# An attention and mixture-of-experts layer on one core: one product moved to GpSimd, GELUs in a row, first scan ahead of the statistics

## The reference

```
x = x + layernorm(linear_attention(layernorm(x)))
x = x + layernorm(moe(layernorm(x)))

linear_attention: q, k, v = x @ W_qkv + b      16 heads of 8; q, k = elu(.) + 1 + 1e-4
    per token t, along the sequence:
    kv_s += k_t (outer) v_t ;  k_s += k_t
    out_t = (q_t . kv_s) / (q_t . k_s + 1e-6)  then @ W_out + b_out

moe: shared = gelu(x @ Wfc_s + b) @ Wproj_s + b          hidden 512
     routed = the two experts of 8 with the largest softmax(x @ Wr), each
              gelu(x @ Wfc[e] + b) @ Wproj[e] + b, weighted by their probabilities
```

## Time and profile before

| | us |
|---|---|
| median of 3 runs (lowest, highest) | 401.99 (401.25, 403.97) |
| the profiled execution, its own time | 400.21 |
| its span in the profile | 398.4 |
| TensorE busy in the span | 338.0 (85%) |
| VectorE busy | 303.1 (76%) |
| ScalarE busy | 262.3 (66%) |
| GpSimd busy | 247.9 (62%) |

### The profile page before, as it was taken

The page is one execution under the profiler, slowest core; times in us unless marked ns, Lnnn a source line. Parts: engine busy times, 40 slices in busy tenths (PEclk is TensorE's granted clock), DMA queues, the critical chain, the costliest instruction groups (busy, mean ns, idle before and its releaser), DMA issues.

```text
span 398.4 us, 8675 instructions
## 1 busy us (share of the span) xinstructions
PE 338.0 (85%) x2551; PEld 298.5 (75%) x2551; DVE 303.1 (76%) x737; ACT 262.3 (66%) x665; POOL 247.9 (62%) x338
## 2 busy tenths in 40 slices
PE   6648489698787896977989789999999999999990
PEld 2326458587576684965958689999999999997990
DVE  5699999898998989989999447766656666662283
ACT  4758474885967849679473797556666666664682
POOL 6851282575885747748547577777766666667061
PEclk9959779999999999999999999999999999999995
DMA  7563986248074340611501897999898888821883
GB/s 198 173 160 96 213 155 204 61 120 226 8 224 115 98 139 0 203 34 61 177 3 46 251 314 219 248 280 289 266 318 250 243 248 251 255 95 54 248 273 113
DMA packets 53493, 69.03 MB, mean 173 GB/s; under 512 B 6349, under 2 KB 37370, under 8 KB 53466
## 3 DMA queue, kind: packets, MB, share of 16 engines
q1 hardware_dynamic: 48628, 59.11, 52.7%
q0 software_dynamic: 4544, 9.35, 7.0%
q10 hardware_dynamic: 294, 0.26, 0.3%
HBM read 40.06 MB, written 18.15 MB: 146 GB/s over the span
## 4 chain that ended last, share of the span: by engine, by line
PE 43%; ACT 18%; DVE 11%; issue 9%; DMA 7%; POOL 5%; SPq 4%; ACTq 1%; DVEq 0%; POOLq 0%
PE bO L1304 7%; PE bS L1304 6%; PE bO L1116 5%; DVE KV L1448 4%; DMA xb<-expert_lists 3%; ACT xn L722 2%; POOL expert_lists L599 2%; DVE KV L1442 2%; ACT shared L722 2%; ACT shared L768 2%; ACT shared L737 2%; ACT SH L996 2%; PE bV L1279 2%; PE bV L1280 2%; PE bV L1281 2%
## 5 line engine op out<-in xcount | busy, mean ns | idle before, releaser
L687 POOL DMA_INDIRECT expert_results<-yb,yrow x78 | 84.2, 1080 | 34.6 <-issue 18.5
L599 POOL DMA_INDIRECT expert_lists<-rows,pos x64 | 66.4, 1037 | 21.0 <-issue 21.0
L1448 DVE TENSOR_TENSOR_SCAN KV<-bS,KV 128x1024 f32<-128x1024 bf16 x32 | 72.4, 2263 | 0.0
L1116 PEld LDWEIGHTS bO<-wout_rot,Z 128*128 128x128 f32 x512 | 60.2, 192 | 5.8 <-issue 2.3
L1116 PE MATMUL bO<-wout_rot,Z 128*128 128x128 f32 x512 | 61.4, 275 | 2.0 <-DVE Z L1458 1.1
L1767 DVE COPY yrow<-xb 128x2 int32<-128x2 int32 x39 | 9.5, 245 | 43.1 <-PE bO L1304 24.4
L1442 DVE TENSOR_TENSOR KV<-bV,vr 128x1024 f32<-128x1024 f32 x32 | 38.7, 1214 | 2.8 <-DMA vr<-vr 2.8
L1088 PEld LDWEIGHTS bA<-w2s_sb,hs 128*128 128x128 f32 x256 | 31.6, 191 | 8.7 <-ACT hs L833 7.3
L1088 PE MATMUL bA<-w2s_sb,hs 128*128 128x128 f32 x256 | 34.1, 280 | 3.8 <-ACT hs L833 3.7
L953 ACT ACTIVATE hs<-bV,KV 128x256 f32<-128x256 f32 x56 | 22.0, 478 | 17.3 <-PE bV L1281 17.3
L1458 DVE TENSOR_TENSOR Z<-KV,shared 128x1024 f32<-128x1024 f32 (+1 forms) x24 | 28.9, 1231 | 0.0
(11 more groups left out here) (358 smaller groups left out, 977.5 us busy)
## 6 DMA issues: line engine op xcount, KB each, us to landing
KV<-packed_weights SPq DMA_DIRECT2D x21, 578.0 KB
Z<-packed_weights SPq DMA_DIRECT2D x18, 578.0 KB, 4.8
xb<-expert_lists SPq DMA_DIRECT2D x39, 129.0 KB
vr<-vr SPq DMA_DIRECT2D x16, 224.0 KB
vr<-vr SPq DMA_DIRECT2D x16, 192.0 KB
vr<-vr SPq DMA_DIRECT2D x16, 160.0 KB
vr<-vr SPq DMA_DIRECT2D x16, 128.0 KB
packed_weights<-in_L_ffn_Wfc SPq DMA_DIRECT2D x8, 256.0 KB, 5.2
```

What stands on the lines that cost most here:

```text
L599: g.indirect_dma_start(out=lists, out_offset=bass.IndirectOffsetOnAxis(ap=pos[:, m:m + 1], axis=0), in_=rows[:, m // TILES, m % TILES, :], ...
L687: g.indirect_dma_start(out=results, out_offset=bass.IndirectOffsetOnAxis(ap=yrow[n][:, c], axis=0), in_=yb[n][:, c, :], in_offset=None).th ...
L1116: ins = t.matmul(bO[:, j * D:(j + 1) * D], Z[:, d, j * P:(j + 1) * P], wout_rot[:, d], start=False, stop=True, skip_group_check=True)
L1448: v.tensor_tensor_scan(w, ps_keep, w, 0.0, ALU.mult, ALU.add).then_inc(s["kv_sum"], 1)
```

## The change

Its parts are:

- GpSimd takes the product of value rows 6 and 7 (`last_pair`) in each attention round, ahead of `sum_of_x1`. It can't read PSUM, so ScalarE copies the keys to SBUF first (`copy_keys`), after VectorE's second product, into a buffer that is free by then (`keys`). VectorE's third product and GpSimd's wait for that copy, the last scan for GpSimd.
- VectorE's first scan stands right behind the second product, ahead of the statistics.
- ScalarE does the four GELUs in a row, then the spread reciprocals, then the attention norm. Before, the norm and the spread reciprocals stood between the third and the fourth.
- On TensorE the denominators come ahead of projection 0, FC chunk 3 ahead of the projections, the transposes of the reciprocals after two projections, and ranks after the third.
- In rounds 0 and 1 (`FREE = 2`) GpSimd does the second pair of Z too (`second_zed`). In round 0 the filling of padding moves behind it, and so does the subtraction that makes `w1s_lo`, which VectorE had in round 1. `zeds` and `z1s` are the counts that fit this.

```diff
@@ GpSimd
+            def last_pair(i):
+
+                pool.wait_ge(s["k_copied"], i + 3)
+                if from_on(i, 1):
+                    pool.wait_ge(s["z_ready"], zeds(i - 1, 3))
+                pool.wait_ge(vr_in[3], 64 * (i + 1))
+                g.tensor_tensor(KV[:, 6:8], keys.unsqueeze(1).broadcast_to([P, 2, STEP]), vr[:, 6:8], ALU.mult
+                                ).then_inc(s["kv_last"], 1)
+
+            def second_zed(i):
+
+                pool.wait_ge(s["kv_sum"], 4 * i + 2)
+                g.tensor_tensor(Z[:, 2:4], KV[:, 2:4], qn[:].unsqueeze(1).broadcast_to([P, 2, STEP]), ALU.mult
+                                ).then_inc(s["z1_ready"], 1)
...
                     inv_std0_early()
-                    fill_pads()
-                    means_late()
                 if nxt and routed:
                     route_gaps(i)
                     route_chosen(i)
+                if head:
+                    last_pair(i)
+                if isinstance(i, int) and i == 0:
+                    means_late()
...
                     g.tensor_tensor(Z[:, 1], KV[:, 1], qn[:], ALU.mult).then_inc(s["z1_ready"], 1)
+                    if isinstance(i, int) and i < FREE:
+                        second_zed(i)
+                if isinstance(i, int) and i == 0:
+                    fill_pads()
+                    rest_of_weights()
@@ ScalarE
+            def copy_keys(st):
+
+                act.wait_ge(s["kv_prod"], 3 * st + 2)
+                a.activation(keys, bK[:], ACT.Copy).then_inc(s["k_copied"], 1)
...
+                if routed:
+                    rest_of_x(i)
+                if head and from_on(i, 1):
+                    copy_keys(i)
                 if routed and nxt:
-                    rest_of_x(i)
...
-                    gelus(i - 2, 0, 3, pair_h)
+                    gelus(i - 2, 0, CH, pair_h)
                 elif routed:
-                    rest_of_x(i)
-                    gelus(i - 2, 0, 3, pair_h)
-                if tail:
-                    attention_out(i)
+                    gelus(i - 2, 0, CH, pair_h)
                 act.wait_ge(s["den_inv"], i + 1)
...
                 a.activation(rden8[:], rden[:].unsqueeze(2).broadcast_to([P, TILES, E, H]), ACT.Copy
                              ).then_inc(s["rden_ready"], 1)
+                if tail:
+                    attention_out(i)
                 if nxt:
                     ln0_apply(i + 1)
-                if routed:
-                    gelus(i - 2, 3, 4, pair_h)
@@ TensorE
                     fc(i - 2, 1, ga, pair_h[1])
-                    proj(i - 2, 0)
                 if head:
...
                 if routed:
                     fc(i - 2, 2, ga, pair_h[2])
+                    fc(i - 2, 3, ga, pair_h[3])
+                    proj(i - 2, 0)
                     proj(i - 2, 1)
-                    fc(i - 2, 3, ga, pair_h[3])
-                    proj(i - 2, 2)
-                    pe.wait_ge(s["gelu_done"], CH * (i - 2) + 3)
-                    ranks(i)
...
                     ins.then_inc(s["exp_done"], 1)
+                if routed:
+                    proj(i - 2, 2)
+                    ranks(i)
+                    proj(i - 2, 3)
                 if nxt:
                     ln0_transposes(i + 1)
-                if routed:
-                    proj(i - 2, 3)
@@ VectorE
+                if pair == 2:
+                    dve.wait_ge(s["k_copied"], i + 3)
...
             def sums(i, part):
-                dve.wait_ge(s["kv_prod"], E // 2 * i + part + 1)
+                if part == 3:
+                    dve.wait_ge(s["kv_last"], i + 1)
+                else:
+                    dve.wait_ge(s["kv_prod"], 3 * i + part + 1)
...
                     prod(i, 0)
                     prod(i, 1)
+                    sums(i, 0)
                 if tail:
...
-                if head:
-                    sums(i, 0)
                 if routed:
                     route_hot(i)
...
                     v.scalar_tensor_tensor(out=qn[:], in0=q0[:], scalar=FEAT_EPS, in1=bB[:], op0=ALU.add,
                                            op1=ALU.mult).then_inc(s["qn_ready"], 1)
-                    prod(i, 3)
...
-                    zed(i, 1)
+                    if from_on(i, FREE):
+                        zed(i, 1)
```

60 lines of the change are left out of this document (33 added, 27 removed).

## The result

| | kernel before | changed kernel |
|---|---|---|
| median of the runs | 402.41 us (4 runs, 401.25 to 403.97) | 410.25 us (4 runs, 408.17 to 411.65) |
| ratio, with its 95% interval | | 1.0188 [1.0128, 1.0248] |
| profiled execution, its span | 400.21, 398.4 us | 408.17, 406.4 us |
| mean granted TensorE clock of that execution | 0.963 | 0.938 |

The changed kernel is 1.9% slower. The prediction had 400.6 us and a range up to 404.0; the measured time lies above it. Some executions of a kernel fall into a slower state, and every ratio and interval here goes by the others alone, so a ratio can differ from the quotient of two medians.

What follows compares the result with a forecast made beforehand. VectorE, the fullest engine, and ScalarE were taken to bound the attention rounds in two loops of almost one length. Terms -0.5 + 0 + 2.6 - 0.7 gave 1.4 us gained: 400.6 us as a median, range 396.8 to 404.0.

Steps and rivals of the forecast that it cites:

- Round 1's running sum: After round 0's output products on TensorE: starts at 37.3 instead of 39.01, 1.7 us gained.
- GpSimd's product: The 128x1024 product in each attention round: taken as 2.5 us, bounded by 1.3 and 5.0.
- pos waiting for placed: VectorE in steady rounds: third scan done at 153.1, pos not before 155.0, a new wait of 1.9 us for GpSimd.
- the steady rounds: Rounds 4 to 6: 24.7 us each, against 25.43 and 25.65 before.
- The saving of 2.6 us for rounds 4 to 6: Sum over three steady rounds: 0.7 + 0.95 + 0.95 us gained.
- the transposes start at 151.4 instead of 152.54: ScalarE's loop is 1.14 shorter: Round 5, TensorE and ScalarE: the fourth GELU no longer stands behind the next norm; ScalarE's loop becomes 24.5 us.
- The start of round 3: After rounds 0 to 2: about 85.1 instead of 84.68, 0.5 us lost up to there.
- the second norm's factors 2.2 us late on GpSimd: Start of round 2: GpSimd has them at 61.0, ScalarE wants them at 58.6; 1.5 us of the lateness reaches TensorE.
- Round 3 itself: Taken as 0: 0.6 us lost if its wait for value rows recurs, 1.0 gained if not.
- Round 7: VectorE's logits copy put off by 2.0 us behind the scan, delaying norm, scatters and first block's rows: 0.7 us lost.
- the collision of the earlier trace: VectorE with two SBUF inputs and GpSimd reading SBUF exclude one another: GpSimd's power takes 1.85 us beside Z, 1.04 alone.
- a gain of 1.4 us: Whole kernel: -0.5 + 0 + 2.6 - 0.7 us, from rounds 0 to 2, 3, 4 to 6 and 7; chance 0.47.

Runs made afterwards that it cites:

- the zeros: Changed kernel plus ten 512-column products of zeros on TensorE between ln0's transposes and the projections; 402.35 us, ratio 0.9991, beside 403.0 for the kernel before.
- before_unrolled: Kernel before with rounds 3 to 6 written out in place of the device loop; 402.66 us, ratio 0.9981.
- product_only: Changed kernel with ScalarE's and TensorE's orders as before; product on GpSimd, earlier first scan and setup edits stay; 458.18 us, ratio 0.9862.
- before_again: Kernel before, unchanged, profiled on a third chip of the experiments; 461.94 us, ratio 0.997.

## Why the prediction was wrong

**What held.** Round 1's running sum starts at 37.20 (predicted 37.3), and the multiply behind it is stretched. GpSimd's product takes 2.36 us (2.5 from twice a half). The estimate with the Trainium skill (GPSIMD Engine Reference, "Elementwise — side-by-side cycle accounting") was 2.35, and the trace agrees. Statistics behind the scan, the reciprocal at 147.25, the fourth GELU at 147.16, the norm at 148.37, pos waiting for placed with 1.17 in round 5 (1.9 predicted): the frame of a round is as worked out. With the clock kept, the steady rounds are 24.33 to 24.55 us, somewhat better than the 24.7 of the sum. The saving of 2.6 us for rounds 4 to 6 was then 3.46.

**The step that failed** is "the transposes start at 151.4 instead of 152.54: ScalarE's loop is 1.14 shorter". The transposes did start earlier, 151.81. The step took the three projections behind them over at 1.10, 1.02 and 1.02 us without looking at what stood around them. The change had moved a piece of 1.16 us out of the gap between transposes and projections. The idle stretch of 1.72 became 2.79, the clock halved, and the three took up to 2.7 us more: more than the 1.14 gained. The prediction costed that move at nothing and did not mention the clock, which its show at 1.00. No rival had it. The Trainium skill (TensorE: Matmul & The Clock Gate, "HAM oscillation — how this bites in real kernels") tells of waits for transfers between groups of products, each of which puts the array back to its low clock for the next group. It has no price for a kernel whose TensorE is 85% busy. The table above shows the same fall, with waits of 2.79 us for ScalarE; read as a warning, the page would have asked for a look at the gap.

In numbers: rounds 4 to 6 were to give 2.6 and cost 1.21, an error of 3.8 us. Round 7's start, forecast at 2.1 us sooner (a loss of 0.5 up to round 3, then the 2.6), came 1.54 later. On the other chip like the study's the zeros moved it from 190.78 to 183.52.

**The start of round 3** came out at 85.05, as predicted (85.1), but only in part for the reason given. The prediction had the second norm's factors 2.2 us late on GpSimd; the norm at 59.57 did wait for them, 0.91 us. The trace has slow projections there too (4.92 us in sum), and with the zeros the changed kernel starts it at 83.95 to 85.25, in six traces on five chips. The two were not taken apart, so the right number is in part luck.

**Round 3 itself** was taken at zero change and is 25.72 for 25.76, the one round whose clock held.

**Round 7** was to lose 0.7 us, and from its start to the second block's rows it lost 3.36. The chain up to the scatters lost little more than forecast: the last scatter starts 31.93 us behind the round's start, before 30.84. The missing 2.3 us are the last scatter's landing, 4.80 instead of 2.54 up to the load of the first rows. The prediction followed GpSimd up to its scatters, but put no transfer beside them: the last scatter moved by 2.63 us, the weights load by only 1.38, and the load came from 1.37 us behind the scatter's start to 0.12. That this is what held the scatter up is argued from the traces, not shown by an edit. Nor did the prediction follow TensorE into the wait for the blocks' first rows, where the late rows cost it the clock once more (5.09 us in place of 3.65).

Of the 1.09 us by which the last scatter starts later in the round, 0.64 lie between the first and the last of the eight (11.15 us from start to start, before 10.51). The first one began beside a Z of VectorE. The rows of GpSimd, then VectorE:

```profile
209.49 2.58 POOL L609 DMA_INDIRECT expert_lists<-rows,pos  x1 [0.59 <-issue]
212.37 0.96 POOL L609 DMA_INDIRECT expert_lists<-rows,pos  x1 [0.30 <-issue]
```

```profile
209.37 1.73 DVE L1513 TENSOR_TENSOR Z<-KV,shared 128x1536 f32<-128x1536 f32 x1
```

It took 2.58 us, where its neighbour takes 0.96, and ended 0.97 behind that Z's end. It has the look of the collision of the earlier trace rows, met by a scatter. The kernel before had smaller ones (1.65 and 1.75 us for its second and fourth scatter), and the reading was not tested by itself.

**The sign.** The forecast was a gain of 1.4 us. The zeros, which remove only the slow projections, bring the changed kernel to 402.35 beside 403.0, a difference that this measurement does not tell from none. What the late scatter costs at the end on such a chip was not measured.

## What to carry to other kernels

When an edit moves work on TensorE, write down the idle stretches of before and after it as well as the work: taking filler out of a wait ahead of a group of products can lower the clock for much of the group, and that price comes behind the gain and on the critical path. Here 1.16 us of filler left the gap, and 2.3 us of zeros in it brought back 7.5 us of 410. If the order is worth having, a few products of zeros in the gap are a cheap test, and may be the fix. When a chain moves later by a microsecond or two, ask which large transfer now starts beside it, and what TensorE's longer wait does to its clock.

## What was not expected of the hardware

The clock fell for a difference of 1.07 us of idleness (1.72 to 2.79), and between the two the answer was mixed: at 1.72 (before_unrolled, product_only) and at 1.90 one execution had full and lowered rounds. In round 5 the lowered clock lasted through the group and into the next product, which took 0.63 us at 160.51 where it took 0.38 before; in other rounds it rose within the group (2.05, 1.53 and 1.02 us at the end of round 6).

One and the same pair of kernels had different signs on different chips: 1.0188 and 1.0185 on two chips where the kernel before takes 402 to 403 us, 0.9887 and 0.9862 (the last with an interval up to 1.0005) on two where it takes 461 and 468. On the latter kind three engines stop together for 4 us and more a round while transfers run. The trace puts the longest of these waits down to another core or an unknown queue (7.9 us of ScalarE in round 6 of before_again), which names nothing, and its cause is open. Four of the five chips of the experiments were of that kind, so a ratio of 1 to 2% from one chip says little about another.
